# A 3x3 convolution between mixture layers: its result goes to the token layout by SBUF-to-SBUF DMAs, a block of 14 rows each

## The chip, the cores and the metric

The kernel runs on one core of a Trainium2 chip. The metric is the device time of one execution in microseconds; the median of several runs is given. Everything is float32 on the outside. Matrix products are made from float32r pairs, a high part and the rest, so that each product takes three matmuls.

## What is computed

The input x has 2 batches, 8 channels (one per expert), 256 rows and 256 columns. Three layers are expert MLPs, one is a 3x3 convolution over the channels. Each normalises its input over groups of two channels and adds its result to x.

```python
x = x + mlp(_gn(x), L0 ...)          # per channel e: gelu(x[e] @ w1[e] + b1[e]) @ w2[e] + b2[e]
x = x + conv3x3(_gn(x), L1 ...)      # 8 -> 8 channels, edge padding, weights sign(w) * mean|w|
x = x + mlp(_gn(x), L2 ...)
x = x + mlp(_gn(x), L3 ...)          # exact gelu

def _gn(v, G=4, eps=1e-05):          # mean and variance of each (batch, pair of channels)
    g = v.reshape(B_, G, C_ // G, H_, W_)
    m = jnp.mean(g, axis=(2, 3, 4), keepdims=True)
    s = jnp.var(g, axis=(2, 3, 4), keepdims=True)
    return ((g - m) / jnp.sqrt(s + eps)).reshape(v.shape)
```

## The kernel before

**Two layouts.** The MLPs work on XT, which holds x with the image column d (the MLP's feature) on the partitions: XT[d mod 128, d div 128, batch, channel, n]. It stays in SBUF for the whole kernel. The convolution works on XC, which has 16 neighbouring rows of all 8 channels on the 128 partitions (partition = row within the block times 8 plus channel, free axis 256 positions and 2 of padding). Its "rows" are the index d of XT. A block of XC takes 16 rows in and gives 14 rows out (OUTR), so 256 rows need 19 blocks (NBLK) per batch; the last one gives the last 4 rows only. Two blocks make a tile, 10 tiles per batch (TILES), 20 in all, numbered q.

**Into XC.** During layer 0, SP's queue stores each finished channel of XT to a DRAM tensor x1 (store_x1, L391 to L400) and loads it into XC in overlapping blocks (load_xc, L402 to L419: the line L412 loads 14 partitions, 8 apart, with 18 rows of 1 KB each).

**The convolution.** For each tile GpSimd normalises (L514), ScalarE makes the high part (L632), VectorE the low part (conv_low, L909), TensorE runs six matmuls against a band matrix (L1137), ScalarE scales in PSUM (L637), and VectorE adds the result into XC in place (conv_add, L918, semaphore cadded). The matmuls of tile q wait for the sum of tile q - 4, because four PSUM banks are used in turn.

**Out of XC.** SP waits for each tile's sum and stores its two blocks to a second DRAM tensor x2 (L455, 256 KB, 128 partitions). After the tiles 5, 7, 9 and 9 again (GROUPS) it waits for the stores of a group of blocks and reads them back into XT (read_x2, L442 to L447), where a partition gets 8 KB (8 channels of 256). pieces_back joins whole blocks of one chunk of 128 partitions into a single DMA: up to 6 blocks, 672 KB. Seven reads per batch bring home 19 blocks. The reads of batch b count on the semaphore x2_in[b].

**Who needs it.** Layer 2 begins with the statistics of the first two channels, separately for each batch. VectorE waits for all of x2_in[0] (L945) while three tiles are still to be summed for good, does the sums, and goes on with the rest of the convolution's tiles, mixed with the steps of the normalisation (L943 to L962): bn_stats L668, bn_aggr L675, a mean over partitions by matmul (L1010), L682 to L686, a second matmul for the variance (L1016), L692, GpSimd's power (L508), L701, then the normalised input L724 and its low part L729. TensorE's order is fixed too: the mean's matmul stands before tile 18, the variance's before tile 19. Then comes layer 2, whose first two experts are run in halves, batch 0 of both and then batch 1 of both. The statistics of batch 1 (job 10) are made at the first step of expert 1's batch-0 half; VectorE waits for x2_in[1] there (L835).

**The MLP.** Per step TensorE does six matmuls for the hidden tile (L1031) and six for the output of an earlier step (L1049, L1050, L1054); ScalarE applies gelu (L574) and makes the high part (L578), VectorE the low part Hl (L735). The weights of the next expert are split meanwhile (ScalarE L561, VectorE L714). SP loads weights with L361 (w1) and L365 (w2); the loads for expert 2 of layer 2 and later stand behind all stores and reads of x2 on SP's queue (L461 to L463).

Of the kernel before, what the change touches and what calls it, by code (L numbers as in the profile page):

```python
# [24 lines left out]
F32 = mybir.dt.float32  # L25
# [5 lines left out]
B, C, N, D, H = 2, 8, 256, 256, 1024  # L31
PART = 128
# [11 lines left out]
ROWS = PART // C  # L44
OUTR = ROWS - (KS - 1)
NBLK = -(-D // OUTR)
LASTROW = D + 2 - ROWS
NP = N + 2
DP = D + 2
TILES = -(-NBLK // 2)  # L50
CRING = 3


GROUPS = [(6, 5), (10, 7), (16, 9), (NBLK, TILES - 1)]
STORED = [end for end, tile in GROUPS]


def pieces_back():


    pieces = []
    for k in range(NBLK):
        d, end = OUTR * k, min(OUTR * (k + 1), D)
        j = d - LASTROW + 1 if k == NBLK - 1 else 1
        while d < end:
            c = d // PART
            n = min(end, (c + 1) * PART) - d
            if k not in STORED and pieces and n == OUTR and pieces[-1][3] == OUTR and pieces[-1][4] == c:
                k0, blocks, j0, nj, c, p0 = pieces.pop()
                pieces.append((k0, blocks + 1, j0, nj, c, p0))  # L70
            else:
                pieces.append((k, 1, j, n, c, d % PART))
            d, j = d + n, j + n
    return pieces


HALVED = (C - 1, C, C + 1)
# [8 lines left out]
def order(P):  # L86

    if isinstance(P, int) and 2 * P in CROSSED:
        return [(ee, b * HT + t) for b in range(B) for ee in range(2) for t in range(HT)]
    return [(ee, t) for ee in range(2) for t in range(units(2 * P + ee if isinstance(P, int) else None))]  # L90
# [91 lines left out]
def known(value):  # L182

    return value if isinstance(value, int) else -1
# [30 lines left out]
def build(nc, x, w1, b1, w2, b2, cw, cb, out):  # L215

    x1_dram = nc.dram_tensor("x1_scratch", (C, DP, TOK), F32, kind="Internal").ap()
    x2_dram = nc.dram_tensor("x2_scratch", (B, NBLK, ROWS, C, N), F32, kind="Internal").ap()

    with ExitStack() as ctx:  # L220
        def sb(name, shape, dt=F32, where=ctx):
            return where.enter_context(nc.sbuf_tensor(name, shape, dt))
# [4 lines left out]
        def sem(name):  # L227
            return ctx.enter_context(nc.semaphore(name))


        XT = sb("XT", [PART, DC, B, C, N])
# [49 lines left out]
        XC = sb("XC", [PART, B, NBLK, NP])  # L281
# [3 lines left out]
        with ExitStack() as use:  # L285
# [31 lines left out]
        cst_done, pads = sem("cst_done"), sem("pads")  # L317
        cn_done, chi, clo, conv_mm, cscaled, cadded = (sem("cn_done"), sem("chi"), sem("clo"), sem("conv_mm"),
                                                       sem("cscaled"), sem("cadded"))
        x2_out = [[sem(f"x2_out{b}_{n}") for n in range(len(STORED))] for b in range(B)]  # L320
        x2_in = [sem(f"x2_in{b}") for b in range(B)]
        out_tr, out_evac = sem("out_tr"), sem("out_evac")
        out_st = [sem(f"out_st{b}") for b in range(B)]
# [23 lines left out]
        def evacuated(i):  # L347

            return (in_evac_dve, i // 2 - 2) if i % 2 == 0 else (in_evac_act, i // 2 + 3)
# [3 lines left out]
        def _(sp):  # L353
# [13 lines left out]
            for i in range(2 * B):  # L367
                e, b = divmod(i, B)
# [54 lines left out]
            for E in range(2, C + 1):  # L423
                f, e = divmod(E, C)
# [12 lines left out]
                    load_w1(1, 1, C + 1)  # L437
                    load_w2(1, 1, C + 1)

            def read_x2(b, n):  # L440

                sp.wait_ge(x2_out[b][n], 16 * (-(-STORED[n] // 2) - (STORED[n - 1] // 2 if n else 0)))  # L442
                for k, blocks, j, nj, c, p0 in pieces_back():
                    if k < STORED[n] and (n == 0 or k >= STORED[n - 1]):
                        sp.dma_start(XT[p0:p0 + blocks * nj, c, b],  # L445
                                     x2_dram[b, k:k + blocks, j:j + nj].rearrange("k j o n -> k j (o n)")
                                     ).then_inc(x2_in[b], 16)  # L447


            for b in range(B):  # L450
                for i in range(TILES):
                    sp.wait_ge(cadded, b * TILES + i + 1)
                    own = slice(2 * i, min(2 * i + 2, NBLK))
                    n = sum(2 * i >= end for end in STORED)
                    sp.dma_start(x2_dram[b, own].rearrange("k j o n -> (j o) k n"), XC[:, b, own, 1:N + 1]  # L455
                                 ).then_inc(x2_out[b][n], 16)
                    for n, (end, tile) in enumerate(GROUPS):
                        if i == tile:
                            read_x2(b, n)

            with sp.Fori(2, C) as e:  # L461
                load_w1(1, e, C + e)
# [193 lines left out]
        def _(dve):  # L656
# [13 lines left out]
            def sums_done(J, late=False):  # L670
                wait(dve, bn_done, 2 * (jobs_weighed(J, late) + len(batches(J))))
# [132 lines left out]
            def pair(P, f):  # L804
                for ee, t in order(P):
                    E, e = 2 * P + ee, 2 * (P - NPAIR * f) + ee
                    jobs, norms = jobs_of(P, ee, f), norms_of(P, ee, f)
                    for J, steps, src, slot in jobs:
                        if steps.get("aggregate") == t and steps["sums"] != t:
                            sums_done(J, f > 0)  # L810
                    if known(E) in CROSSED and t % HT == 2:
                        if (ee, t) != (0, 2):
                            evict(E - 1 if ee else E + 1, 1 - ee, 1 - ee, f, t // HT if ee else 0)
                    elif known(E) == C + 2 and t == 2:
                        evict(E - 1, 1, e - 1, f, 1)
                    elif t == 2 and known(E) != 0:
                        if known(E) == 2 * C:
                            evict(E - 1, 1 - ee, C - 1, 1)
                        else:
                            evict(E - 1, 1 - ee, e - 1, f)  # L820
                    elif t == HT + 2:
                        evict(E, ee, e, f, 0)
                    h_lo(E, t, f)
                    if known(E) == 0 and t in (1, 3):
                        x_evac(4 + t)
                    k = split_at(P, ee, t)
                    if k is not None:
                        w_lo(E + 1, 1 - ee, k)
                    for J, steps, src, slot in jobs:
                        if steps.get("sums") == t:  # L830
                            if known(E) == 0:
                                for i in (7, 8):
                                    dve.wait_ge(*evacuated(i))
                            if known(J) == 10:
                                dve.wait_ge(x2_in[1], 16 * len(pieces_back()))  # L835
                            if known(J) == 7:
                                dve.wait_ge(evicted, evicts(C) - DC)
                            elif f == 0 and ee:
                                wait(dve, evicted, evicts(2 * P, 0))
                            elif known(P) == 7 or f == 2:  # L840
                                wait(dve, evicted, evicts(2 * P - 4, 1))
                            sums(J, src, (0,) if "more_sums" in steps else None)
                        if steps.get("more_sums") == t:
                            sums(J, src, (1,))
                        if steps.get("aggregate") == t:
                            if steps["sums"] == t:
                                sums_done(J, f > 0)
                            aggregate(J)
                        if steps.get("deviate") == t:
                            deviate(J)  # L850
                        if steps.get("eps") == t:
                            add_eps(J)
                        if steps.get("scale") == t:
                            scale_shift(J, slot)
                    if t + 1 in norms:
                        En, b, J = norms[t + 1]
                        norm(En, En % C if isinstance(En, int) else e + 1, b, J)
                    if t in norms:
                        En, b, J = norms[t]
                        x_lo(En, En % 2 if isinstance(En, int) else 1 - ee, b)  # L860
                    if known(E) == 1 and t % 2 == 1:
                        x_evac(8 + t)
                    if known(E) == 1 and t == 6:
                        signs_and_means()
                    if known(E) == C - 2 and t in (2, 6):
                        band(1 if t == 2 else 2)
                    if known(E) == C - 1 and t == 14:
                        dve.wait_ge(st_done, 8)
                        to_partitions(0)


            for i in range(4):
                e, b = divmod(i, B)
# [68 lines left out]

            q = B * TILES  # L943
            conv_low(q - 3)
            dve.wait_ge(x2_in[0], 16 * len(pieces_back()))  # L945
            sums(9, 0)
            sums_done(9)
            aggregate(9)
# [229 lines left out]
```

## Time and profile before

| | |
|---|---|
| median of 3 runs | 631.81 us (631.55 to 632.73) |
| span of the profiled execution | 629.2 us |
| TensorE busy | 596.4 us (95%) |
| VectorE busy | 423.5 us (67%) |
| ScalarE busy | 430.6 us (68%) |
| GpSimd busy | 31.4 us (5%) |
| mean granted TensorE clock | 0.981 |
| DMA moved | 77.78 MB, 124 GB/s in the mean |

Layer 0 runs to about 203 us, the convolution to about 250 us, layers 2 and 3 to the end. The page's slices show TensorE at 90% or more in nearly every slice; the two exceptions beyond the start lie at slices 14 and 16, between 230 and 275 us. The median of the runs is 2.6 us above the profiled execution's span. Times of one instruction are in microseconds in the timelines and nanoseconds in the groups; a bracket at the end of a timeline's row is the engine's idle time before that instruction and what ended it.

### The profile page before, as it was taken

What the parts mean: (1) busy time and instruction counts of PE and PEld (TensorE: products, weight loads), DVE (VectorE), ACT (ScalarE), POOL (GpSimd) and SP (SyncE); (2) the same over time, 40 slices, a digit from 0 to 9 for tenths busy, and PEclk for the clock granted to TensorE, in tenths of its full rate; (3) what the DMA queues carried; (4) which work ended last, traced back from release to release, by engine and by line L of the source; (5) the groups of instructions that cost most, each with busy time, mean ns of one, the idle gap of its engine ahead of it and who ended that gap; (6) DMA issues with size and microseconds to landing.
All of it is one profiled execution on the core that took longest, in us unless ns stands there. A gap on an engine that the chain in (4) does not pass through costs nothing.

```text
span 629.2 us, 9514 instructions
## 1 busy us (share of the span) xinstructions
PE 596.4 (95%) x2973; PEld 503.7 (80%) x2973; DVE 423.5 (67%) x857; ACT 430.6 (68%) x741; POOL 31.4 (5%) x52
## 2 busy tenths in 40 slices
PE   8999999999999974959999999999999999999997
PEld 7778888888898753859988888888888888888885
DVE  4777967866795965546876767856855865765632
ACT  5767667767776762726977767767776767777753
POOL 2000000000001540000000000000000000000000
PEclk9999999999999996979999999999999999999999
DMA  8762464445545654630423232231423424334001
GB/s 269 201 213 100 141 174 141 128 145 148 184 121 165 202 180 160 185 71 2 134 67 135 67 111 91 72 129 67 133 68 102 150 85 132 118 86 152 30 18 67
DMA packets 57500, 77.78 MB, mean 124 GB/s; under 512 B 3942, under 2 KB 50806, under 8 KB 56950
## 3 DMA queue, kind: packets, MB, share of 16 engines
q1 hardware_dynamic: 57462, 77.31, 39.1%
q8 instruction: 19, 0.31, 0.2%
q14 instruction: 19, 0.16, 0.1%
HBM read 63.90 MB, written 13.40 MB: 123 GB/s over the span
## 4 chain that ended last, share of the span: by engine, by line
PE 82%; DMA 8%; DVE 5%; issue 2%; POOL 1%; ACT 1%; SPq 1%; DVEq 0%; POOLq 0%; ACTq 0%
PE G L1031 40%; PE ACC L1054 13%; PE ACC L1049 13%; PE ACC L1050 13%; DMA XT<-x_scratch 3%; DMA x_scratch<-XC 3%; DMA W2raw<-in_L_conv_w 1%; DVE Cl L909 1%; DVE XC L918 1%; DVE BN L668 1%; PE TR L1067 1%; DMA W1raw<-in_L_conv_w 1%; PE TR L997 1%; PE STAT L1010 0%; SPq L445 0%
## 5 line engine op out<-in xcount | busy, mean ns | idle before, releaser
L735 DVE TENSOR_TENSOR Hl<-HR,Hh 128x512 fp32r<-128x512 f32 (+1 forms) x216 | 136.2, 630 | 160.0 <-ACT Hh L578 158.6
L574 ACT ACTIVATE HR<-G,BT 128x512 f32<-128x512 f32 (+1 forms) x216 | 138.5, 641 | 146.7 <-PE G L1031 145.5
L1031 PE MATMUL G<-Xh,W1l 128*128 128x512 f32 (+1 forms) x432 | 164.2, 380 | 3.4 <-issue 2.0
L1031 PE MATMUL G<-Xl,W1h 128*128 128x512 f32 (+1 forms) x432 | 159.1, 368 | 0.0
L1031 PE MATMUL G<-Xh,W1h 128*128 128x512 f32 (+1 forms) x432 | 159.0, 368 | 0.0
L1049 PE MATMUL ACC<-Hh,W2l 128*128 128x512 f32 (+1 forms) x432 | 156.7, 367 | 0.0
L1050 PE MATMUL ACC<-Hh,W2h 128*128 128x512 f32 (+1 forms) x432 | 156.4, 367 | 0.0
L578 ACT ACTIVATE Hh<-HR 128x512 fp32r<-128x512 f32 (+1 forms) x216 | 126.3, 585 | 8.7
L1054 PE MATMUL ACC<-Hl,W2h 128*128 128x512 f32 (+1 forms) x432 | 123.4, 367 | 0.3 <-DVE Hl L735 0.3
L1031 PEld LDWEIGHTS G<-Xh,W1l 128*128 128x128 f32 x432 | 82.5, 191 | 15.6 <-issue 2.2
L1031 PEld LDWEIGHTS G<-Xh,W1h 128*128 128x128 f32 x432 | 82.3, 191 | 13.5
L1049 PEld LDWEIGHTS ACC<-Hh,W2l 128*128 128x128 f32 x432 | 82.1, 190 | 13.4
L1050 PEld LDWEIGHTS ACC<-Hh,W2h 128*128 128x128 f32 x432 | 82.1, 190 | 13.2
L1031 PEld LDWEIGHTS G<-Xl,W1h 128*128 128x128 f32 x432 | 82.6, 191 | 11.5
L1054 PEld LDWEIGHTS ACC<-Hl,W2h 128*128 128x128 f32 x432 | 78.2, 189 | 14.1 <-DVE Hl L735 0.9
L714 DVE TENSOR_TENSOR W2l<-W2raw,W2h 128x512 fp32r<-128x512 f32 x96 | 65.6, 685 | 3.6 <-ACT W2h L561 2.9
L714 DVE TENSOR_TENSOR W1l<-W1raw,W1h 128x512 fp32r<-128x512 f32 x96 | 65.5, 685 | 1.7 <-ACT W1h L561 1.4
L561 ACT ACTIVATE W2h<-W2raw 128x512 fp32r<-128x512 f32 x96 | 58.8, 615 | 3.0 <-DMA W2raw<-in_L_conv_w 3.0
L561 ACT ACTIVATE W1h<-W1raw 128x512 fp32r<-128x512 f32 x96 | 58.6, 616 | 1.1 <-DMA W1raw<-in_L_conv_w 1.1
L668 DVE BATCH_NORM_STATS2 BN<-XT 128x6 f32<-128x512 f32 (+1 forms) x60 | 37.3, 680 | 19.5 <-DMA XT<-x_scratch 19.5
L508 POOL TENSOR_TENSOR RS<-VE,half 128x2 f32<-128x2 f32 (+1 forms) x18 | 12.8, 710 | 506.2 <-DVE VE L692 506.2
L729 DVE TENSOR_TENSOR Xl<-XN,Xh 128x512 fp32r<-128x512 f32 x48 | 32.9, 685 | 0.3
(73 smaller groups left out, 359.6 us busy)
## 6 DMA issues: line engine op xcount, KB each, us to landing
W1raw<-in_L_conv_w SPq DMA_DIRECT2D x24, 1024.0 KB, 5.0
W2raw<-in_L_conv_w SPq DMA_DIRECT2D x24, 1024.0 KB, 5.6
x_scratch<-XC SPq DMA_DIRECT2D x18, 256.0 KB, 2.8
x_scratch<-XT SPq DMA_DIRECT2D x16, 256.0 KB
out_x<-OUTT SPq DMA_DIRECT2D x16, 256.0 KB, 2.2
XC<-x_scratch SPq DMA_DIRECT2D x16, 252.0 KB
NAT<-in_x SPq DMA_DIRECT2D x6, 512.0 KB, 8.4
XT<-x_scratch SPq DMA_DIRECT2D x4, 672.0 KB
```

Source lines behind the costliest of these rows:

```text
L508: nc.gpsimd.tensor_tensor(RS[:, bs], VE[:, bs], half[:, bs], ALU.pow).then_inc(rs_done, 1)
L561: nc.scalar.activation(dst, src, ACT.Copy).then_inc(whi, 1)
L574: nc.scalar.activation(HR[:, t % 2, 0:n], G1[t % 2][:, 0:n], func, bias=BT[:, bass.ds(col, 1)]).then_inc(gelu_done, 1)
L578: nc.scalar.activation(Hh[:, t % RING, 0:n], HR[:, t % 2, 0:n], ACT.Copy).then_inc(hhi, 1)
L668: nc.vector.bn_stats(BN[:, b, i], at).then_inc(bn_done, 1)
L714: nc.vector.tensor_tensor(dst, src, high.bitcast(F32), ALU.subtract).then_inc(wlo, 1)
L729: nc.vector.tensor_tensor(Xl[:, par, :, b], XN[:, b], Xh[:, par, :, b].bitcast(F32), ALU.subtract).then_inc(xlo, 1)
L735: nc.vector.tensor_tensor(Hl[:, t % RING, 0:n], HR[:, t % 2, 0:n], Hh[:, t % RING, 0:n].bitcast(F32), ALU.subtract).then_inc(hlo, 1)
L1031: ins = nc.tensor.matmul(G1[t % 2][:, 0:width(b)], w[:, ee, c, col], rhs, start=n == 0, stop=n == len(parts) - 1)
L1049: nc.tensor.matmul(banks[m][:, 0:n], W2l[:, ee, t8, col], high, start=t8 == 0, stop=False)
L1050: nc.tensor.matmul(banks[m][:, 0:n], W2h[:, ee, t8, col], high, start=False, stop=False)
L1054: ins = nc.tensor.matmul(banks[m][:, 0:n], W2h[:, ee, t8, col], Hl[:, t % RING, 0:n], start=False, stop=t8 == HT - 1)
```

## The change

The DRAM tensor x2, its semaphores x2_out, the groups and the joined reads are gone. After each tile's sum SP issues, for each of the tile's blocks, a DMA that reads the block's 14 rows out of XC (112 partitions of 1 KB) and writes them into XT (14 partitions of 8 KB). Block 9 crosses from chunk 0 to chunk 1 of XT and takes two DMAs (2 rows and 12 rows); the last block has 4 rows. That makes 20 DMAs per batch. The waits on x2_in are for the same event, with the new count.

```diff
+def rows_back(k):
+
+    d, end = OUTR * k, min(OUTR * (k + 1), D)
+    j = d - LASTROW + 1 if k == NBLK - 1 else 1
+    parts = []
+    while d < end:
+        c = d // PART
+        n = min(end, (c + 1) * PART) - d
+        parts.append((j, n, c, d % PART))
+        d, j = d + n, j + n
+    return parts
...
-            def read_x2(b, n):
-
-                sp.wait_ge(x2_out[b][n], 16 * (-(-STORED[n] // 2) - (STORED[n - 1] // 2 if n else 0)))
-                for k, blocks, j, nj, c, p0 in pieces_back():
-                    if k < STORED[n] and (n == 0 or k >= STORED[n - 1]):
-                        sp.dma_start(XT[p0:p0 + blocks * nj, c, b],
-                                     x2_dram[b, k:k + blocks, j:j + nj].rearrange("k j o n -> k j (o n)")
-                                     ).then_inc(x2_in[b], 16)
+            def give_back(b, k):
+
+                for j, nj, c, p0 in rows_back(k):
+                    sp.dma_start(XT[p0:p0 + nj, c, b].rearrange("p o n -> p (o n)"),
+                                 XC[j * C:(j + nj) * C, b, k, 1:N + 1]).then_inc(x2_in[b], 16)
...
             for b in range(B):
                 for i in range(TILES):
                     sp.wait_ge(cadded, b * TILES + i + 1)
-                    own = slice(2 * i, min(2 * i + 2, NBLK))
-                    n = sum(2 * i >= end for end in STORED)
-                    sp.dma_start(x2_dram[b, own].rearrange("k j o n -> (j o) k n"), XC[:, b, own, 1:N + 1]
-                                 ).then_inc(x2_out[b][n], 16)
-                    for n, (end, tile) in enumerate(GROUPS):
-                        if i == tile:
-                            read_x2(b, n)
+                    for k in range(2 * i, min(2 * i + 2, NBLK)):
+                        give_back(b, k)
```

## Rows read from the trace of the kernel before

**Rows 1.** Waits: engine and line, waited for; us in total, times, longest.
```profile
DVE BN L668 <- DMA XT<-x_scratch: 19.5, 2, 10.9
PE STAT L1010 <- DVE MV L675: 19.4, 2, 11.5
```

**Rows 2.** Chain that ended last, 222 to 272 us: start us, us, what.
```profile
222.36 9.88 DMA x_scratch<-XC
...
232.95 8.46 DMA XT<-x_scratch
...
251.50 7.37 DMA x_scratch<-XC
...
259.57 12.73 DMA XT<-x_scratch
```

**Rows 3.** Timeline of VectorE: start us, us, line, operation, [idle before].
```profile
221.92 0.41 DVE L918 TENSOR_TENSOR XC<-ACC,XC 128x256 f32<-128x256 f32 x1
...
241.43 1.29 DVE L668 BATCH_NORM_STATS2 BN<-XT 128x6 f32<-128x512 f32 x2 [10.95 <-DMA XT<-x_scratch]
...
246.62 0.16 DVE L692 TENSOR_SCALAR VE<-STAT 128x1 f32<-128x1 f32 x1 [1.52 <-PE STAT L1016]
...
249.67 1.01 DVE L918 TENSOR_TENSOR XC<-ACC,XC 128x512 f32<-128x512 f32 x2
250.60 2.49 DVE L714 TENSOR_TENSOR W1l<-W1raw,W1h 128x512 fp32r<-128x512 f32 x4
253.00 0.42 DVE L735 TENSOR_TENSOR Hl<-HR,Hh 128x256 fp32r<-128x256 f32 x1
...
272.32 1.29 DVE L668 BATCH_NORM_STATS2 BN<-XT 128x6 f32<-128x512 f32 x2 [8.54 <-DMA XT<-x_scratch]
```

**Rows 4.** Timeline of TensorE's matmuls, 243 to 274 us.
```profile
243.01 0.59 PE L1010 MATMUL STAT<-MV,ones_mean 128*128 128x1 f32 x2 [11.49 <-DVE MV L675]
...
249.85 0.36 PE L1031 MATMUL G<-Xh,W1l 128*128 128x256 f32 x1 [2.05 <-issue]
...
254.04 0.41 PE L1054 MATMUL ACC<-Hl,W2h 128*128 128x256 f32 x2
...
273.90 0.59 PE L1010 MATMUL STAT<-MV,ones_mean 128*128 128x1 f32 x2 [7.95 <-DVE MV L675]
```

**Rows 5.** Windows, TensorE alone: stretch, us, busy, clock, DMA share, GB/s.
```profile
69.75:70.50 0.75, 0.75 (x5) 1.00 0.83 280
226.50:231.50 5.00, 5.00 (x22) 1.00 0.35 128
240.00:243.00 3.00, 0.00 (x0) 0.50 0.13 46
243.00:247.00 4.00, 3.99 (x12) 0.50 0.48 145
250.50:253.90 3.40, 3.40 (x19) 0.51 0.68 245
271.00:277.70 6.70, 3.79 (x17) 0.50 0.16 55
```

**Rows 6.** View by tile, DMA issues on SP: ns least/median/most, first and last.
```profile
L455 SPq DMA_DIRECT2D x_scratch<-XC x20: 359/387/2325, 211.2 to 251.5; - x20
...
L412 SPq DMA_DIRECT2D XC<-x_scratch x16: 860/869/943, 64.9 to 208.3; - x16
...
L445 SPq DMA_DIRECT2D XT<-x_scratch x14: 300/646/823, 216.4 to 259.6; - x14
```

**Rows 7.** Page, DMA issues: count, KB each, median us from issue to landing.
```profile
x_scratch<-XC SPq DMA_DIRECT2D x18, 256.0 KB, 2.8
```

**Rows 8.** Timeline of SP's queue: start us, us, line.
```profile
210.62 0.52 SPq L419 DMA_DIRECT2D XC<-x_scratch  x1
...
260.43 0.43 SPq L361 DMA_DIRECT2D W1raw<-in_L_conv_w  x1
```

**Rows 9.** Timeline of ScalarE, layer 2: the first weight split of expert 2.
```profile
297.49 0.61 ACT L561 ACTIVATE W1h<-W1raw 128x512 fp32r<-128x512 f32 x1
```

More of the change, by code:

```diff
@@ L51 @@
 CRING = 3
-GROUPS = [(6, 5), (10, 7), (16, 9), (NBLK, TILES - 1)]
-STORED = [end for end, tile in GROUPS]
-def pieces_back():
[L61 to L74, printed above, removed]
+def rows_back(k):
[8 more added lines that the diff above has]
+    return parts
+def pieces_back():
+    return sum(len(rows_back(k)) for k in range(NBLK))
 HALVED = (C - 1, C, C + 1)
@@ L217, in build @@
     x1_dram = nc.dram_tensor("x1_scratch", (C, DP, TOK), F32, kind="Internal").ap()
-    x2_dram = nc.dram_tensor("x2_scratch", (B, NBLK, ROWS, C, N), F32, kind="Internal").ap()
     with ExitStack() as ctx:
@@ L319, in build @@
                                                        sem("cscaled"), sem("cadded"))
-        x2_out = [[sem(f"x2_out{b}_{n}") for n in range(len(STORED))] for b in range(B)]
         x2_in = [sem(f"x2_in{b}") for b in range(B)]
@@ L834, in pair @@
                             if known(J) == 10:
-                                dve.wait_ge(x2_in[1], 16 * len(pieces_back()))
+                                dve.wait_ge(x2_in[1], 16 * pieces_back())
                             if known(J) == 7:
@@ L944, in _ @@
             conv_low(q - 3)
-            dve.wait_ge(x2_in[0], 16 * len(pieces_back()))
+            dve.wait_ge(x2_in[0], 16 * pieces_back())
             sums(9, 0)
```

## The prediction

> **What bounds the kernel now.** I read the list of waits first. It holds one pair that matters: VectorE's statistics of layer 2's input (L668) wait 19.5 us for the read back of the convolution's result, in two waits, and TensorE waits 19.4 us for what follows from them [rows 1]. Everywhere else the list has at most 2.0 us a group for TensorE's matmuls, so a microsecond taken from these two waits is a microsecond off the time, as long as nothing else is late behind them.
>
> The chain of work shows what each wait consists of: for batch 0 the store of the last block (9.88 us to land), then the issue of the reads that waited for it, then the last read (8.46 us); for batch 1 the same with 7.37 and 12.73 us [rows 2]. These are two trips through DRAM in series, behind other traffic on the same queue. VectorE's timeline gives the clock times. The last of the ten tiles of batch 0 is summed at 222.33 us (start 221.92 plus 0.41). VectorE then works on batch 1 up to 230.48, has nothing left to do before the statistics, and starts them at 241.43 (10.95 us idle). The second time it would be ready at 263.78 and starts at 272.32 (8.54 us idle) [rows 3]. TensorE's timeline shows idle times of 11.49 and 7.95 us at the same places [rows 4].
>
> The windows give two more things. The granted clock is 0.50 while TensorE sits idle and stays there after it resumes: in 243 to 247 us, again in 250.5 to 253.9 us, and in 271 to 277.7 us [rows 5]. So each wait costs more than its idle time. And in 240 to 243 us, at the end of the first wait, the DMA engines are only 13% busy at 46 GB/s, about two engines out of 16 (23 GB/s each); in 226.5 to 231.5 us they are 35% busy at 128 GB/s, about six engines [rows 5]. The reads that join 2 or 6 blocks in one transfer run on that few engines.
>
> **Removed: store and read back.** Twenty stores and fourteen reads leave SP's queue, and with them both serial trips. What remains between the last sum of a batch (L918) and the statistics is the issue of the last blocks' DMAs and their landing.
>
> **Added: 40 DMAs.** Nineteen blocks per batch, with block 9 in two parts because it crosses from chunk 0 to chunk 1: 20 per batch. A whole block reads 112 partitions of 1 KB from XC and writes 14 partitions of 8 KB into XT, 112 KB. No transfer from SBUF to SBUF is in the trace, so two costs have to be bounded.
>
> *Issue on SP.* The reads of L445 took 0.30 to 0.82 us to issue; the loads of L412, which also have 14 rows and 252 pieces of 1 KB, 0.86 to 0.94 us; the stores of L455 mostly 0.36 to 0.39 [rows 6]. The new DMA has the 14 rows of the L412 form but fewer pieces. I take 0.65 us, and keep 0.30 and 0.94 as ends.
>
> *Transfer and landing.* The load of L412's form moved data at 280 GB/s with the engines 83% busy in 69.75 to 70.50 us [rows 5], and the 256 KB stores land in 2.8 us in the median [rows 7]. At 280 GB/s a block takes 0.4 us; at the 128 GB/s of the six-engine read it takes 0.9 us. I take 0.4, so that the issue is what spaces the DMAs, and 2.3 us from the last issue's end to the landing (a smaller transfer than the store), with 2.8 as the upper end.
>
> **Batch 0.** SP is busy with the loads of XC until 211.14 us [rows 8], so no give-back can go out earlier. From there 20 issues of 0.65 us end at 224.2 us, which is after the last tile's 222.33; landing at 226.5. VectorE comes to the wait at 230.48, so 4.0 us are spare and the 10.95 us go entirely. The point from which this fails is (230.48 - 2.3 - 211.2)/20 = 0.85 us per issue; at 0.94 the wait would be 1.8 us. At 0.30 us the last tile would set the landing, which changes nothing. What hides the 20 issues is the convolution of both batches that runs on until 230.5; were it absent they would be the path, 13 us long.
>
> **Batch 1.** Five of its tiles are summed before VectorE reaches the statistics, the other five behind them, the last 9 us after these, at 250.7 [rows 3], so about 238.2 after the shifts of the first wait (10.95 + 1.5). SP follows the tiles and is done near 240, landing 242.3. VectorE wants the data at 263.78 minus the shifts so far (10.95 + 1.5 + 0.6), 250.7. Spare: 8.4 us. Even at 0.94 us per issue all forty are landed at 211.2 + 37.6 + 2.3 = 251.1, against 252.5 (the first wait is then 1.8). So the second wait goes too, and TensorE's 7.95 us with it.
>
> **What is moved behind them.** On SP the weight loads L361 and L365 for the third expert of layer 2 stand behind the give-backs. They now go out near 240 to 243 instead of 260.43 [rows 8], and ScalarE splits the first of them at 297.49 [rows 9], about 275 after the shifts; earlier is worth nothing. The new DMAs write XT rows of a batch whose last readers in layer 0 are over, so no wait is added on another engine. What is late next is the ordinary chain statistics, GpSimd power, normalisation, which takes as long as before.
>
> **The clock's part.** In 243 to 247 us TensorE is busy 3.99 us at 0.50, work worth 2.0 us at full clock; VectorE stands still for 1.52 us there for the second statistic [rows 3, 5]. I take 1.5 us of gain. In 250.5 to 253.9 us TensorE works 3.40 us at 0.51, which alone would be 1.7; but the first Hl is computed at 253.00 to 253.42, behind four weight splits on VectorE, and TensorE's matmul of it is at 254.04 [rows 3, 4]. Faster matmuls would gain only 0.6 us there, and this only if the clock stays up over the 2.05 us pause at 249.85, which remains. In 271 to 277.7 us TensorE is busy 3.79 us at 0.50: 1.8 us of gain, for the pause before it is gone.
>
> **The sum.** 10.95 (first wait) + 1.5 + 0.6 + 7.95 (second) + 1.8 = 22.8 us. The profiled execution spans 629.2 us, which gives 606.4; the median of the runs is 631.81, 2.6 us above the span for what lies around it, so the forecast for the median is 609.0 us.
>
> **The rivals.**
>
> *A. The transfers, not the issues, space the DMAs (chance 0.12).* [...] For it: the reads into neighbouring partitions never show more than 128 GB/s in a long stretch; against it: that is explained by their six engines, and the 14-row load reached 280 GB/s [rows 5]. A batch has 2.10 MB. At 128 GB/s this is 16.4 us from about 211.6, landing at 230.1: still hidden. Below that it decides: at 110 GB/s it is 19.1 us, landing at 232.8, a wait of 2.3 us, and perhaps the clock's 1.5 us back: 611.3 to 612.8. [...]
>
> *B. SP's issue costs more than any seen, 0.95 to 1.4 us (0.09).* The two sides have different shapes (14 rows against 112). At 1.1 us batch 0 lands at 235.5, a wait of 5.0 us with the clock's first part back; batch 1 is again nearly hidden: about 616 us.
>
> *C. Slower (0.05).* The new DMA is split over few engines, as the joined reads are. At 23 GB/s per engine [rows 5] a block on two engines takes 2.45 us. Batch 0 lands near 258.5 instead of 241.4 and batch 1 near 303.4 instead of 272.3: 31 us later in all, about 663. It decides from 1.5 us per block, that is fewer than about 3.3 engines (or an issue of 1.5 us). Against it: 14 divides both sides, and the L412 load with 14 rows kept 83% of the engines busy.
>
> *D. Nothing comes of it (0.02):* a case between B and C, near 632.
>
> **How the numbers follow.** Forecast 0.72, A 0.12, B 0.09, C 0.05, D 0.02. A measurement of this kernel can tell about 0.2% (1.3 us) from no change. Faster by more: 0.93; within: 0.02; slower: 0.05. The range for 8 in 10: below, 607.0, if the clock's parts are worth their full 2.0, 1.7 and 1.9 us; above, 614.0, which takes in case A with the clock, the 0.94 us issue, and the light end of B.
>
> **What the changed profile should show.** No wait of L668 for a DMA, or under 2 us; SP's issues of the give-back near 0.65 us each, with the last of batch 0 before 228; TensorE's idle time before STAT near 0.6 us in place of 11.49 and none in place of 7.95; granted clock 1.00 from 230 to 270. Wrong if an issue takes over 0.85 us, if blocks land more than 0.9 us apart with the engines under half busy, or if the clock still falls.

## The result

The changed kernel takes 615.01 us (614.43 to 615.61), the kernel before 632.01 us in the same measurement: a ratio of 0.973, with a 95% interval from 0.971 to 0.975. It is 17 us faster, where 23 were forecast. The range was 607 to 614, so the time lies 1.0 us above it; the prediction was wrong in size, not in sign. The profiled execution spans 612.4 us, 16.8 less than before; its mean granted clock is 0.989.

The list of waits of the changed kernel answers [rows 1]: one wait of VectorE for these transfers is left, of 3.2 us, and TensorE waits 3.7 us for what follows.

```profile
DVE BN L653 <- DMA XT<-XC: 3.2, 1, 3.2
PE STAT L995 <- DVE MV L660: 3.7, 1, 3.7
```

Its chain of work around the first wait answers [rows 2] (start us, us, what). When the last tile of batch 0 is summed, SP is behind and has seven issues of batch 0 to make. Six follow each other at 0.65 to 0.80 us (three of them are left out here), and the transfer of the seventh lands 6.36 us after its issue begins. Then the statistics begin. The chain has no DMA at the second wait.

```profile
222.46 0.35 DVE XC L903
222.81 0.65 SPq L436
223.50 0.80 SPq L436
...
226.88 0.80 SPq L436
227.72 6.36 DMA XT<-XC
234.10 1.30 DVE BN L653 x2
235.68 0.58 PE STAT L995 x2
236.27 2.77 PE ACC L1122 x6
239.25 1.60 PE ACC L1122 x6
240.85 1.95 issue
242.79 3.31 PE G L1016 x18
```

VectorE's timeline answers [rows 3]: 3.16 us idle before the first statistics, none before the second (256.85). Layer 2's first matmul is at 242.79 where it was at 249.85 [rows 4].

```profile
234.10 1.29 DVE L653 BATCH_NORM_STATS2 BN<-XT 128x6 f32<-128x512 f32 x2 [3.16 <-DMA XT<-XC]
...
239.29 0.16 DVE L677 TENSOR_SCALAR VE<-STAT 128x1 f32<-128x1 f32 x1 [1.52 <-PE STAT L1001]
...
256.85 1.28 DVE L653 BATCH_NORM_STATS2 BN<-XT 128x6 f32<-128x512 f32 x2
```

The view by tile gives the issues on SP (ns least, median, most), to be held against [rows 6]: 40 of 0.80 us.

```profile
L436 SPq DMA_DIRECT2D XT<-XC x40: 675/801/890, 211.6 to 245.0; - x40
```

And the windows (stretch, us, TensorE busy, clock, DMA share, GB/s), to be held against [rows 5], show what the transfers do: from 220 to 231 us the share is 0.99, and the engines move only 113 GB/s. The share is the time of all packets divided by that of 16 engines. It can pass 1 (it does in two rows here, and e7 has 1.16), so it is a measure for comparing rows and not a strict percentage. The last two rows are for the clock: 0.51 in both stretches after the wait.

```profile
220.00:231.00 11.00, 10.94 (x48) 1.00 0.99 113
214.00:231.00 17.00, 16.47 (x72) 1.00 0.93 116
234.00:240.50 6.50, 4.82 (x16) 0.51 1.01 110
244.50:247.80 3.30, 3.30 (x15) 0.51 1.05 113
```

So the 17 us can be made up of 7.8 of the first wait's 10.95, the second wait whole (7.95 us of TensorE) and the 1.8 us that the prediction gave for the low clock around it. Against them stand 0.5 us by which the convolution began later in this execution (SP is free for the give-backs at 211.6, not 211.1).

### The profile page after: what moved, and what is told of

It reads as the page before. It is cut to its first block, busy times and chain, and to the rows that moved or that the text cites. A ratio compares the mean times of both kernels' runs of the same rounds, so it can differ in the third digit from the quotient of the medians.

```text
span 612.4 us, 9520 instructions
## 1 busy us (share of the span) xinstructions
PE 594.5 (97%) x2973; PEld 501.0 (82%) x2973; DVE 423.2 (69%) x857; ACT 430.3 (70%) x741; POOL 31.3 (5%) x52
## 4 chain that ended last, share of the span: by engine, by line
PE 87%; DVE 4%; DMA 2%; issue 2%; SPq 2%; POOL 1%; ACT 1%; DVEq 0%; POOLq 0%; ACTq 0%
PE G L1016 42%; PE ACC L1039 14%; PE ACC L1034 14%; PE ACC L1035 14%; DMA W2raw<-in_L_conv_w 1%; DVE Cl L894 1%; DMA XT<-XC 1%; PE TR L1052 1%; SPq L374 1%; DVE XC L903 1%; DVE BN L653 1%; SPq L436 1%; PE ACC L1122 1%; PE TR L982 1%; PE STAT L995 0%
```

## The experiments

Two things were open. Why does a block of 112 KB take so long to land, at a share of 0.99 and at 40% of the rate that the L412 load reached (280 GB/s)? Theory N: the 14 rows go to neighbouring partitions, and the writes to neighbours hinder each other. Theory S: a copy from SBUF to SBUF in pieces of 1 KB is that slow anywhere. And what does the wait cost beyond its own length?

**e1_spread9: the same bytes to partitions 9 apart.**

```diff
-                    sp.dma_start(XT[p0:p0 + nj, c, b].rearrange("p o n -> p (o n)"),
+                    if nj == OUTR:
+                        s = k % 9 if c == 0 else k - 10
+                        rows = slice(s, s + 9 * 13 + 1, 9)
...
+                    sp.dma_start(XT[rows, c, b].rearrange("p o n -> p (o n)"),
                                  XC[j * C:(j + nj) * C, b, k, 1:N + 1]).then_inc(x2_in[b], 16)
```

> The changed kernel with every whole block written to 14 partitions that lie 9 apart instead of 14 neighbours; bytes, sources, number of rows and order of the DMAs are the same, so the rows of XT are permuted (and one row of the last block is left out). What it computes from layer 2 on is therefore another thing, the work is the same. Theory N (neighbouring partitions hinder the 14 engines): the rate in 220 to 231 us rises from 115 to 250 GB/s or more wherever a DMA is in flight, the last block of batch 0 lands within 3 us of its issue at 227.7 (6.4 in the changed kernel), the first wait of the statistics falls from 3.2 to at most 0.5 us, the time by 3 to 6 us, to 609 to 612. Theory S (a copy from SBUF to SBUF in 1 KB pieces runs at this rate wherever it goes): 115 GB/s, wait 3.2 us, 615 us. The issues on SP stay 0.80 us by both.

Measured: 609.67 us, ratio 0.964 (0.963 to 0.966), 5.3 us less than the changed kernel, and 0.7 from the forecast. There is no wait for a DMA in either batch: in the chain the statistics follow VectorE's own work.

```profile
230.43 0.81 DVE Cl L903
231.25 1.21 DVE BN L662 x2
```

The two windows of e1:

```profile
214.00:231.00 17.00, 16.44 (x73) 1.00 0.45 123
220.00:231.00 11.00, 10.94 (x48) 1.00 0.43 117
```

The rate expected (250 GB/s) is not there, because nothing asks for it: 112 KB every 0.85 us are at most 135 GB/s. What tells the two kernels apart is the share. The changed kernel needs 0.99 for 113 GB/s, e1 0.43 for 117. In the trace's packet records of 220 to 231 us a packet of 1 KB takes 144 ns in the median in the changed kernel and 46 ns in e1. The source, the pieces and the path are the same, so theory S falls: the place of the 14 rows is the cause. The issues kept their length (0.81 us in the median), so the long issues by themselves leave no wait.

**e2_spread4: partitions 4 apart.** The edit is that of e1 with steps of 4 in place of 9.

> As e1_spread9, but 14 partitions that lie 4 apart (one block in nine still goes to neighbours), again a permutation of XT's rows. [...] Theory S: 115 GB/s as before.

Measured: 609.84 us in a single run, and in 220 to 231 us:

```profile
220.00:231.00 11.00, 10.95 (x49) 1.00 0.45 122
```

As good as 9 apart: 122 GB/s at a share of 0.45 and 117 at 0.43 would be 271 and 272 GB/s at a share of 1 (an estimate; no window here runs that long at it). So rows 1 apart hinder each other (0.99 for 113 GB/s in the changed kernel) and rows 4 apart do not; steps of 2 and 3 were not tried.

**e3_unjoined and e3b_unjoined: the kernel before, one read per block.**

```diff
-            if k not in STORED and pieces and n == OUTR and pieces[-1][3] == OUTR and pieces[-1][4] == c:
-                k0, blocks, j0, nj, c, p0 = pieces.pop()
-                pieces.append((k0, blocks + 1, j0, nj, c, p0))
-            else:
-                pieces.append((k, 1, j, n, c, d % PART))
+            pieces.append((k, 1, j, n, c, d % PART))
```

> The kernel before (store to DRAM and read back) with its reads no longer joined: one read per block, 14 partitions of 8 KB, 20 per batch, in place of 7. Theory N: while several of these reads are in flight they too run at about 115 GB/s with 14 engines busy, though the source is DRAM and pieces are 8 KB. Theory S: they run at 280 GB/s or more, as DRAM to SBUF transfers do elsewhere. The issue of a 14-row read of one shape on both sides: about 0.5 us; if it is 0.80 the number of rows and not the different shapes is what costs. Time: the last read of batch 0 is issued near 232 as before; by N it lands at about the same 241, 628 to 634; by S near 236, 620 to 626.

> The same kernel as e3_unjoined (store to DRAM and one read of 14 partitions per block), whose profiled execution could not be read. Its time was 616 to 619 us, far below the 628 to 634 that theory N gave with the last read of batch 0 issued at 232. So either the store lands earlier, because the joined reads on 2 to 6 engines had held it up (theory Q: the queue behind few-engine reads was the first trip's cost; then the last store of batch 0 lands in 3 to 5 us in place of 9.9), or the reads run faster than 115 GB/s (against N). The trace tells which: share and GB/s of the DMA engines in 222 to 236 us, and the issue time of a 14-row read.

Measured: 619.08 us (ratio 0.979) and 618.16 (0.977); the rows are from the second. So two trips through DRAM with unjoined reads come within 3 to 4 us of the direct copies. Of the 17 us that the change brought, taking the joined reads apart brings 13 to 14 by itself; the direct copy as such is worth only the rest. The windows of e3b, stores and loads in the first, reads of 14 neighbours from DRAM in the second:

```profile
214.00:218.00 4.00, 3.73 (x17) 1.00 0.81 278
220.00:221.00 1.00, 1.00 (x7) 1.00 0.90 117
```

117 GB/s from DRAM, in pieces of 8 KB, at a share of 0.90: the same slowness without SBUF as a source, as N says. The window is short, but its packets agree: 991 ns in the median for 8 KB, where the joined reads of the kernel before took 309 in 226.5 to 231.5 us. The time was not what the expectation gave with N (628 to 634), for the joined reads had cost more than their own landing. The chain has both trips of batch 0:

```profile
223.58 7.35 DMA x_scratch<-XC
...
231.72 6.13 DMA XT<-x_scratch
```

Theory Q is half right: the last store lands in 7.35 us, not 9.88 [rows 2] and not 3 to 5, the last read in 6.13. The first wait is 6.5 us, and of the second only 0.6 is left. The issue of a 14-row read of one shape is short, and this is what the direct copy is to be held against:

```profile
L441 SPq DMA_DIRECT2D XT<-x_scratch x40: 252/383/1645, 217.3 to 255.0; - x40
```

**e7_sixteen: what an issue costs.**

```diff
-                for j, nj, c, p0 in rows_back(k):
-                    sp.dma_start(XT[p0:p0 + nj, c, b].rearrange("p o n -> p (o n)"),
-                                 XC[j * C:(j + nj) * C, b, k, 1:N + 1]).then_inc(x2_in[b], 16)
+                if k < 16:
+                    p0 = 16 * (k % 8)
+                    sp.dma_start(XT[p0:p0 + 16, k // 8, b].rearrange("p o n -> p (o n)"),
+                                 XC[:, b, k, 1:N + 1]).then_inc(x2_in[b], 16)
```

> What an issue costs. The changed kernel with 16 DMAs per batch of 16 rows each (128 partitions read, 16 neighbours written) in place of 20; the last three blocks of a batch aren't brought back, and rows go to other places, so the output is another. If 14 rows (a number that is not 16) make an issue dear, these take 0.4 us or less, as the stores with 128 partitions on both sides do; if the different shapes of the two sides do (many small reads, few large writes), they take about 0.8 us. [...]

Measured: 609.57 us in a single run, with three blocks fewer but the same 2.1 MB per batch. The view by tile has issues of 0.60 us:

```profile
L437 SPq DMA_DIRECT2D XT<-XC x32: 546/600/622, 211.5 to 238.1; - x32
```

The chain, in which the last one lands 9.95 us after it starts, and a window of the same kernel:

```profile
221.30 9.95 DMA XT<-XC
231.27 1.30 DVE BN L654 x2
```

```profile
224.00:228.00 4.00, 4.00 (x19) 1.00 1.16 121
```

Neither 0.4 nor 0.8: unequal shapes cost (0.60 against 0.36 to 0.39 of the 128-partition stores), and 14 rows cost again (0.80 against 0.60). Fourteen rows of one shape can be cheap (0.38 in e3b, 14 pieces of 8 KB) and dear (0.86 to 0.94 in the loads of L412, 252 pieces of 1 KB [rows 6]), so the number of pieces may count too; no run separates it. The landing repeats N: faster issues only lengthened the queue, at 121 GB/s. At this rate batch 0 is in just after VectorE asks for it (a wait of 0.5 us), which is why the time is near that of e1.

**e4_fill: the clock.**

```diff
                 if q == B * TILES - 2:
+                    stay_busy(13)
                     mean_over_partitions(9)
```

> The changed kernel with 13 filler matmul calls on TensorE (128x128, into a bank that nobody reads then) ahead of the mean's matmul, in the first wait. Theory: part of what the wait costs is the granted clock, which falls to 0.50 in 234 to 240 us and again in 244.8 to 247.6. With fillers the clock stays at 1.00 through tiles 18 and 19; the stretch from the statistics (234.1) to layer 2's first matmul (242.8) shrinks by 1.5 us, and the time by 1.5 to 2.1 us, to about 613.2. If the clock were not what it costs, or the chain on VectorE were, no change (615).

Measured: 612.73 us, ratio 0.969 (0.968 to 0.971), 2.3 us less than the changed kernel. The wait is that of the changed kernel (3.09 us), and the work between the statistics and layer 2's first matmul is the same. First the matmul in the changed kernel, whose statistics start at 234.10, then both rows in e4:

```profile
242.79 0.36 PE L1016 MATMUL G<-Xh,W1l 128*128 128x256 f32 x1 [1.95 <-issue]
```

```profile
234.78 1.29 DVE L653 BATCH_NORM_STATS2 BN<-XT 128x6 f32<-128x512 f32 x2 [3.09 <-DMA XT<-XC]
...
241.86 0.35 PE L1016 MATMUL G<-Xh,W1l 128*128 128x256 f32 x1 [2.05 <-issue]
...
255.24 1.28 DVE L653 BATCH_NORM_STATS2 BN<-XT 128x6 f32<-128x512 f32 x2
```

8.69 us became 7.08. That is 1.6 us, near the 1.5 at which the prediction had priced the step at 243 to 247 us. The granted clock of e4 is 1.00 from 231 to 246 us:

```profile
231.00:246.00 15.00, 11.59 (x76) 1.00 1.01 110
```

So the second fall, at the start of layer 2, is gone too. From the first statistics to those of batch 1 it is 20.46 us, where the changed kernel takes 22.75 (234.10 to 256.85): 2.3 less, the whole gain.

**e5_order, e6_order_fill, e8_defer: other work into the wait.** Behind the wait for batch 0's data VectorE has the sums of five tiles of batch 1 to make (not three, as said of the kernel before); e5 puts two of them ahead.

```diff
             conv_low(q - 3)
+            conv_add(q - 5)
+            conv_low(q - 2)
+            conv_add(q - 4)
+            conv_low(q - 1)
             dve.wait_ge(x2_in[0], 16 * pieces_back())
...
                 ins.then_inc(conv_mm, 1)
+            mean_over_partitions(9)
+            variance_over_partitions(9)
```

e6 adds fillers around these two calls; e8 also takes out the splits ahead of `pair(4, 1)` on ScalarE and VectorE and the two lines of split_at that go with them, so that they are made in expert 0's steps.

> The changed kernel with the order around the wait altered: VectorE takes two low parts and two sums of batch 1's tiles ahead of the wait for batch 0's data instead of behind it, and TensorE runs the matmuls of tiles 18 and 19 before the mean's and the variance's. Theory: what waits at 231 is 3.2 us of landing, and 2.1 us of TensorE's and 2.8 us of VectorE's later work can stand in it. Layer 2's first matmul then comes about 6 us after the statistics (234.1) in place of 8.7: 612 to 613 us. If the give-backs of batch 1, which now start earlier, take rate from those of batch 0 that are still in flight, the landing moves later than 234.5 and the gain is under 1 us.

> e5_order with filler matmuls on TensorE: 4 calls ahead of the mean, 8 behind the variance, while it waits for the first normalised input. Theory: the clock stays at 1.00 over the start of layer 2, worth 0.6 to 1.4 us more than e5_order: 611 to 612. If the first steps of layer 2 are bound by VectorE's and ScalarE's weight splits, nothing more than 0.5 us.

> e6_order_fill with the four splits of w1 of expert 1 (L699 and L546, 2.5 and 2.2 us in a row on VectorE and ScalarE ahead of layer 2's first step) spread over the steps of expert 0. Theory: the first Hl no longer waits for them (0.5 us of idle TensorE and more in the first steps), 1 to 2 us less than e6_order_fill: 609.5 to 611. If ScalarE cannot take a split in each of eight steps (1.5 us of its work per step of 1.44), the gain is lost in steps 4 to 7 and the time is that of e6_order_fill.

Measured: 612.28, 612.45 and 612.39 us. e5 does what was expected: from the statistics to layer 2's first matmul 6.1 us (236.35 to 242.45), 2.6 less, and 2.7 in the time. (Its profiled execution is the longest of its four, 614.88 us; everything in it comes 2.2 us later.) The two others should have brought more, and brought nothing that shows: their runs spread from 610.4 to 614.7 us, wider than the three medians lie apart. The chain of e6 tells where the gain went, and below it are the statistics of batch 1 in e6 and in e8:

```profile
244.76 10.11 DMA XT<-XC
254.89 1.30 DVE BN L653 x2
```

```profile
254.89 1.29 DVE L653 BATCH_NORM_STATS2 BN<-XT 128x6 f32<-128x512 f32 x2 [1.30 <-DMA XT<-XC]
```

```profile
254.75 1.29 DVE L649 BATCH_NORM_STATS2 BN<-XT 128x6 f32<-128x512 f32 x2 [0.25 <-DMA XT<-XC]
```

In both kernels these statistics begin at the landing of batch 1's data, at almost the same time: VectorE waits 1.3 us for it in e6 and 0.25 in e8. In the changed kernel these statistics start at 256.85 without a wait: the slow transfers are hidden there by the time lost before. e5 has no second wait; what it leaves is the clock, 0.50 in 242 to 246 us.

**e9_flat, e10_flat_defer_fill, e11_flat_late: a scratch tensor without the overlap.** One store per tile of 112 partitions, three reads of 128, 96 and 32 partitions per batch.

```diff
+    x2_dram = nc.dram_tensor("x2_scratch", (B, D, C, N), F32, kind="Internal").ap()
...
+                    rows = x2_dram[b, 2 * OUTR * i:2 * OUTR * (i + 1)]
+                    sp.dma_start(rows.rearrange("(k j) o n -> (j o) k n", k=2),
+                                 XC[C:(OUTR + 1) * C, b, 2 * i:2 * i + 2, 1:N + 1]).then_inc(x2_out[b][g], 16)
...
+                c, p0, p1 = ((0, 0, PART), (1, 0, 96), (1, 96, PART))[g]
+                sp.wait_ge(x2_out[b][g], 16 * (5, 3, 2)[g])
+                sp.dma_start(XT[p0:p1, c, b], x2_dram[b, c * PART + p0:c * PART + p1]).then_inc(x2_in[b], 16)
```

e10 adds e8's spreading of the splits (not its order around the wait) and 6 filler calls ahead of layer 2. e11 is e10 with the second read moved behind the last store:

```diff
-                    if i in (5, 8, 9):
-                        read_x2(b, (5, 8, 9).index(i))
+                    for g, tile in enumerate((5, 9, 9)):
+                        if i == tile:
+                            read_x2(b, g)
```

> Through DRAM again, but with a scratch tensor of 256 rows without the blocks' overlap: one store per tile (112 partitions, 10 per batch), and 3 reads per batch, of 128, 96 and 32 partitions, the first two issued while the convolution runs. [...] The last store is issued at about 222.8, lands in 3 us, the last read (256 KB) lands in 3 to 4 us more: about 229.5, ahead of 231. No wait for a DMA in either batch, time 608.5 to 611, below both kernels. If two trips through DRAM cost what they did before (7 to 10 us each), the waits come back and it is 620 or more.

> e9_flat with the four splits of w1 of expert 1 spread over expert 0's steps and 6 filler matmul calls between the convolution and layer 2's first matmul. With no DMA left on the path, the clock's fall at the start of layer 2 and the 2.5 us of splits ahead of the first Hl are next: 0.5 to 2 us less than e9_flat. If ScalarE is full in those steps, no gain.

> e10_flat_defer_fill with the second read (96 partitions) issued behind the last store instead of ahead of it. In e9 and e10 SP waited 4 to 6 us for the second group's stores to land before it issued the last tile's store, at 225.96. Theory: it is this wait on SP, not the DRAM trips themselves, that left 3 to 4 us of waiting for the statistics. The last store now goes out at about 223.3, lands near 228, the last read near 231.5: a wait of at most 1 us, 2.5 to 3.5 us less than e10: 609.3 to 610.3 us, with no second wait. If the large read ahead of the last one holds it up instead, the landing stays near 234 and the time at 612.5.

Measured: e9 614.72 us (ratio 0.971), above the 608.5 to 611 expected, and no different from the 615.01 of the direct copies. SP itself stood in a wait: before the second read, until tile 7's store had landed, and only then issued the last store (chain of e9):

```profile
221.38 4.20 DMA x_scratch<-XC
225.60 0.32 SPq L452
225.96 4.86 DMA x_scratch<-XC
230.84 3.37 DMA XT<-x_scratch
234.24 1.30 DVE BN L669 x2
```

e10 takes 612.74 us, 2.0 less for splits and fillers, and has a wait of 3.9. e11 takes 609.90 us, ratio 0.965 (0.964 to 0.966), as expected. Its chain:

```profile
223.71 2.63 DMA x_scratch<-XC
226.36 6.22 DMA XT<-x_scratch
232.61 1.30 DVE BN L666 x2
```

The last store starts at 223.71, and a wait of 0.8 us is left. e11 is the fastest of the kernels that bring every row back to its place, 5.1 us below the changed kernel, and it goes through DRAM. Not all of the 5.1 us is due to the path: e11 also has the spread splits and the fillers, which had brought 2.0 from e9 to e10. The direct copy with both and with the new order (e8) takes 612.39, 2.5 more than e11. The path of e11 without splits and fillers was not run.

## Why the prediction was off

- **The bound and the second wait.** Right. Both waits were the place, and the second went entirely (8.54 to 0), with TensorE's 7.95 us; with the 1.8 us given for the clock there the sum closes. Nothing else came late behind it.
- **Issue on SP.** Taken as 0.65 us, measured 0.80, within the ends (0.30 to 0.94). The last issue of batch 0 ended at 228.5, not 224.2. This alone was harmless: e1 has the same issues and no wait.
- **Transfer and landing.** This is the step that failed. It put 0.4 us per block and 2.3 us for the landing, by the 280 GB/s of the L412 load; measured were 113 GB/s at a share of 0.99, about 1.0 us per block, and 5.6 us from the end of the last issue to the landing. So not the issues but the transfers spaced the blocks. The load had been chosen for its form of 14 rows; but its rows lie 8 apart. Nor was the row at the other end a better choice, though its 128 GB/s came close and it too writes neighbouring partitions: at a share of 0.35 it was rightly put down to its six engines (0.35 of 16), and its packets were not slow (309 ns for 8 KB, against 991 in e3b). That 128 lies near 113 is chance. The trace of the kernel before has no long stretch of the slow kind.
- **Rival A** was the right mechanism, at 0.12. Its 110 GB/s is in no row of the kernel before; the runs showed 113 GB/s in the changed kernel, 117 from DRAM (e3b) and 121 for 16 rows (e7). It gave a wait of 2.3 us at 110 GB/s; the wait was 3.16. The difference is not in the rate: from 211.6 to 234.1 us at some 114 GB/s the engines moved 2.6 MB, and batch 0 has only 2.1. So some engines were on batch 1 while others still had rows of batch 0; this is an estimate worked out from the bytes, not seen row by row. Rival A gave 611.3 to 612.8 us in all.
- **The clock.** The prediction took 1.5 + 0.6 us as gained. Both depended on the first wait's going entirely; with 3.7 us of idle TensorE the clock fell again (0.51 in 234 to 240.5 us) and neither was gained. e4 shows their size: 1.6 us to the first matmul, 2.3 in the time. The second part did not hang on the wait alone: in e1, without the wait, the clock still fell to 0.69 in 238 to 242 us.
- **The sum.** 22.8 less 3.16 of wait, less 2.1 for the clock, less 0.5 for the later start, is 17.0. e1, where transfers no longer space the blocks, takes 609.67 against the forecast 609.0.
- **The range** ended at 614.0 and held case A with the clock's first part at 612.8. It had not put both parts of the clock on top of A, though both follow from one late landing: 609.0 with the wait of 3.16 and the clock's 2.1 is 614.3, and 0.5 for the later start makes 614.8.

## What to carry to other kernels

A DMA's cost depends on which partitions it reaches, not only on its bytes and its number of engines: fourteen neighbours took 2.4 times the engines' time of fourteen rows spread out (a share of 0.99 for 113 GB/s against 0.43 for 117). When a new transfer must be priced by a row of the trace, look where the row's partitions lie, and at its share beside its GB/s: 128 GB/s at 0.35 and 113 at 0.99 are different things. If no row has partitions like those of the new transfer, the price is open, and the range has to say so. Before a path is replaced, its cheap repair is worth a run: reads no longer joined brought 13 to 14 of the 17 us. And a detour through DRAM that gathers many rows into one transfer can match the direct copy (e9) and, with splits and fillers on both sides, beat it by 2.5 us (e11 against e8), if no wait on the issuing queue stands ahead of the last store.

## What the runs showed of the hardware

- Blocks of 14 neighbouring partitions moved at 113 GB/s with a share of 0.99, from DRAM at 117 with 0.90; rows 4 and 9 apart at 122 with 0.45 and at 117 with 0.43. A packet of 1 KB took 144 ns in the median to neighbours and 46 to rows 9 apart.
- A DMA whose two sides have different shapes (112 or 128 small reads into 14 or 16 large writes) took 0.80 and 0.60 us to issue; one of 14 rows with one shape on both sides took 0.38 in 14 pieces, and 0.86 to 0.94 in 252.
- The clock differed with the length of the wait: 3.7 us of idle TensorE before the mean's matmul were followed by a granted clock of 0.51 in 234 to 240.5 us, and 0.5 us of it (e1) by 1.00 up to 238 us. A fall near the start of layer 2 came in runs without fillers (0.69 in 238 to 242 us of e1, 0.51 in 244.5 to 247.8 of the changed kernel, 0.50 in 242 to 246 of e5), and also in e6 with them (0.57 in 238 to 242), but not in e4 (1.00 in 231 to 246).
